# DLRM tower with compressed interaction layers: the first period in two halves of its samples

## The reference

```python
e = jnp.stack([tbl_f[ids[:, f]] for f in range(32)], axis=1)      # 1024 x 32 x 16
x0 = xk = e
for W in (W0, W1, W2):                                            # m x h x 64
    xk = jax.nn.relu(jnp.einsum('bmd,bhd,mhk->bkd', x0, xk, W))
    outs.append(jnp.sum(xk, axis=2))
h = jnp.concatenate([*outs, dense_ctx], axis=1)
h = relu(h @ W_top1 + b_top1); h = relu(h @ W_top2 + b_top2); y = h @ W_top3
```

## Time and profile before

| | |
|---|---|
| median of 3 runs | 638.52 us |
| the profiled execution | 638.18 us |
| its span, first to last instruction | 636.4 us |
| VectorE busy | 579.8 us, 309 instructions |
| TensorE busy | 584.7 us |
| GpSimd busy | 444.7 us, without the gaps between its gathers |
| ScalarE busy | 366.3 us |
| mean DMA rate | 166 GB/s |

### The profile page before, as it was taken

The page is one execution under the profiler, slowest core; times in us unless marked ns, Lnnn a source line. Parts: engine busy times, 40 slices in busy tenths (PEclk is TensorE's granted clock), DMA queues, the critical chain, the costliest instruction groups (busy, mean ns, idle before and its releaser), DMA issues.

```text
span 636.4 us, 7868 instructions
## 1 busy us (share of the span) xinstructions
PE 584.7 (92%) x2896; PEld 209.6 (33%) x2896; DVE 579.8 (91%) x309; ACT 366.3 (58%) x607; POOL 444.7 (70%) x416
## 2 busy tenths in 40 slices
PE   0078899999898989999999999999999999999998
PEld 0023233333232323333334323333334323334355
DVE  1039899999999999999999999999999999999995
ACT  0006474767656565747676575747676575737551
POOL 6677787698888878886979688886989582703012
PEclk9999999999999999999999999999999999999999
DMA  6296598938293845749291846648391946600000
GB/s 172 46 323 143 231 231 257 326 64 295 73 262 129 220 188 123 286 75 334 49 302 62 222 185 147 263 95 314 59 320 38 238 166 150 257 4 1 1 2 1
DMA packets 31315, 105.83 MB, mean 166 GB/s; under 512 B 8774, under 2 KB 14028, under 8 KB 27052
## 3 DMA queue, kind: packets, MB, share of 16 engines
q1 hardware_dynamic: 23084, 103.21, 51.6%
q0 software_dynamic: 8192, 2.11, 2.5%
HBM read 89.56 MB, written 15.73 MB: 165 GB/s over the span
## 4 chain that ended last, share of the span: by engine, by line
DVE 52%; PE 26%; issue 12%; DMA 5%; POOL 2%; SPq 1%; ACT 1%; DVEq 0%; ACTq 0%
DVE prod L555 51%; PE accb L648 9%; PE acca L648 8%; DMA rows<-field_dram 3%; POOL emb L417 2%; PE spread L691 2%; PE acc L605 2%; DMA field_dram<-zb_field 1%; PE accb L669 1%; PE acc L669 1%; SPq L318 1%; DVE prod L536 1%; PE spread L686 1%; ACT zb_field L778 0%; PE spread L612 0%
## 5 line engine op out<-in xcount | busy, mean ns | idle before, releaser
L417 POOL DMA_INDIRECT emb<-in_table,idx x256 | 246.4, 963 | 79.8 <-issue 67.8
L648 PE MATMUL acca<-prod,w 128*64 128x512 f32 x1024 | 229.1, 594 | 2.5 <-DVE prod L555 1.7
L648 PE MATMUL accb<-prod,w 128*64 128x512 f32 x960 | 216.1, 596 | 10.6 <-DVE prod L555 10.6
L555 DVE TENSOR_TENSOR prod<-rows,x1a 128x2048 f32<-128x2048 f32 x64 | 145.7, 2278 | 4.9 <-ACT x1a L783 2.5
L555 DVE TENSOR_TENSOR prod<-rows,x1b 128x2048 f32<-128x2048 f32 (+1 forms) x65 | 145.7, 2245 | 2.0 <-PE accb L648 1.4
L555 DVE TENSOR_TENSOR prod<-rows,x2a 128x2048 f32<-128x2048 f32 x64 | 145.6, 2278 | 0.8 <-PE accb L648 0.8
L555 DVE TENSOR_TENSOR prod<-rows,x2b 128x2048 f32<-128x2048 f32 x64 | 145.6, 2277 | 0.0
L648 PEld LDWEIGHTS acca<-prod,w 128*64 128x64 f32 x1024 | 71.7, 137 | 144.6 <-issue 134.3
L648 PEld LDWEIGHTS accb<-prod,w 128*64 128x64 f32 x960 | 65.8, 137 | 153.0 <-issue 113.7
L435 POOL TENSOR_TENSOR prod<-rows,mates 128x1024 f32<-128x1024 f32 x42 | 99.3, 2382 | 6.8 <-DMA rows<-field_dram 6.6
L783 ACT ACTIVATE x1a<-acc 64x512 f32<-64x512 f32 x62 | 35.3, 570 | 114.6 <-PE acc L605 113.9
(11 more groups left out here) (84 smaller groups left out, 309.3 us busy)
## 6 DMA issues: line engine op xcount, KB each, us to landing
rows<-field_dram SPq DMA_DIRECT2D x30, 2048.0 KB, 11.9
field_dram<-zb_field SPq DMA_DIRECT2D x32, 256.0 KB
mates<-field_dram SPq DMA_DIRECT2D x16, 512.0 KB, 4.4
across<-field_dram SPq DMA_DIRECT2D x56, 128.0 KB, 4.5
emb<-in_table,idx POOLq DMA_INDIRECT x256
field_dram<-zb_field SPq DMA_DIRECT2D x32, 128.0 KB
field_dram<-zb_field SPq DMA_DIRECT2D x16, 192.0 KB
rows<-field_dram SPq DMA_DIRECT2D x2, 1024.0 KB, 7.1
```

What stands on the lines that cost most here:

```text
L417: pool.indirect_dma_start(out=emb[q % EMBS][:, j * EMB:(j + 1) * EMB], out_offset=None, in_=table, in_offset=bass.IndirectOffsetOnAxis(ap= ...
L555: nc.vector.tensor_tensor(prod[:, n % RING, t:t + count, :], rows[:, at + t:at + t + count, c * HALF:(c + 1) * HALF], xs, ALU.mult).then_i ...
L648: mm = nc.tensor.matmul(acc[j % 2][side * HID:(side + 1) * HID, :], (w1 if layer == 1 else w2)[:, step, :], prod[:, (made(layer, s, half, ...
```

## The change

Period 0 is cut into two halves of 32 samples (`SPLITS`), each with all 16 `d`, in 512 columns. *Stream 0* and *stream 1* are now these halves. The ids and first rows of period 0 are laid out so that gathers 1 to 8 bring half 0 and 9 to 16 half 1. Each half has its own turning (`turn_first`, four products), copies out (`fields_first`), list (`list_eights`: eight DMAs of pieces of 512 B, four from SP and four from ScalarE's own queue), mates, rows (three DMAs) and five products of layer 0 (128 x 512). The index addition is split, period 0's first.

Slots 0 and 1 are gone: in their place stand 16 units (`FIRST_UNITS`) of one stream each, on TensorE as `outer_alone` in products of 256 columns. Slot 2 now holds (1, 2) and (1, 3); slots 3 to 31 hold what they held. The five products of period 1's layer 0 stand ahead of slot 2, and the turnings of periods 1 and 2 behind the 6th and the 16th unit. The layer 0 of period 2 is summed behind slot 2's last pair instead of in slot 2, that of period 3 one pair later than before; later ones are where they were. Idle products: six behind the first turning, two behind the second, five before slot 2. The host code lays out the ids; the arithmetic is the same. The diff, cut to its core (ScalarE's `split_twice`, `split_changed_over` and `split_by_d` do for a half of period 0 what the `relu_` functions do, in twice as many operations of 256 columns):

```diff
--- before.py
+++ after.py
...
+    SPLITS = 2
+    SPLIT = BT // SPLITS
+    FIRST_GATHERS = GATHERS // SPLITS
+    PIECE = QUAD * SPLIT
+    EIGHTS = [(first + e, 2 * half + j // 8 + e, step, times) for j, count, half, first, step, times in LIST_PARTS
+              for e in range(count // 8)]
...
-    FIRST = [(0, 2), (2, 2), (4, 1), (5, 3)]
+    FIRST = [(0, 2), (2, 3), (5, 3)]
...
+    FIRST_SLOT = 2
+    FIRST_UNITS = ([(1, 0, half, u) for half in range(2) for u in range(UNITS)] +
+                   [(2, 0, 0, u) for u in range(UNITS)] +
+                   [(1, 1, half, u) for half in range(2) for u in range(UNITS)] +
+                   [(2, 0, 1, u) for u in range(UNITS)] +
+                   [(2, 1, half, u) for half in range(2) for u in range(UNITS)])
     def streams(j):
-        if j == 0:
-            return [(1, 0), (1, 1)]
+        if j == FIRST_SLOT:
+            return [(1, j), (1, j + 1)]
         if j == SUBS - 1:
             return [(2, j - 1), (2, j)]
         return [(1, j + 1), (2, j - 1)]
...
-    MADE = [unit for j in range(SUBS) for unit in vector_units(j)]
+    MADE = FIRST_UNITS + [unit for j in range(FIRST_SLOT, SUBS) for unit in vector_units(j)]
...
-    FIELDS_AT = {(0, 3): 2}
-    SUM0 = {}
+    FIELDS_AT = {(FIRST_SLOT, 2): 3}
+    SUM0 = {(FIRST_SLOT, 3): [(k, 2) for k in (*range(L0 - 1), SQUARES, L0 - 1)]}
+    for q in range(4, PERIODS):
+        FIELDS_AT[2 * q - 5, 3] = q
     for q in range(3, PERIODS):
-        FIELDS_AT[2 * q - 5, 3] = q
-    for q in range(2, PERIODS):
-        SUM0[2 * q - 2, 0] = [(k, q) for k in range(3)]
-        SUM0[2 * q - 2, 1] = [(SQUARES, q), (L0 - 1, q)]
+        late = q == 3
+        SUM0[2 * q - 2, late] = [(k, q) for k in range(3)]
+        SUM0[2 * q - 2, 1 + late] = [(SQUARES, q), (L0 - 1, q)]
...
+        def list_eights(queue, h, odd):
+            for first, of, step, times in EIGHTS[odd::2]:
+                to = bass.AP(field_dram.tensor, (h * LENGTH + first * 8) * HALF,
+                             [[PIECE, FIELDS], [step * 8 * HALF, times], [1, PIECE]])
+                part = bass.AP(zb_field[:, :].tensor, FIELD * N + h * HALF + of * PIECE,
+                               [[N, FIELDS], [0, times], [1, PIECE]])
+                queue.dma_start(to, part).then_inc(s_listed_first[h], 16)
...
+            def list_first(h):
+                sp.wait_ge(s_field, h + 1)
+                list_eights(sp, h, 0)
+                sp.wait_ge(s_listed_first[h], len(EIGHTS) * 16)
+            def mates_first(h):
+                part = bass.AP(field_dram.tensor, (h * LENGTH + MATES) * HALF, [[HALF, P], [1, HALF]])
+                sp.dma_start(mates[:, h * HALF:(h + 1) * HALF], part).then_inc(s_mates, 16)
+            def rows_of_half(h, g):
+                t, count = FIRST[g]
+                part = bass.AP(field_dram.tensor, (h * LENGTH + t) * HALF, [[HALF, P], [1, count * HALF]])
+                sp.dma_start(rows_first[:, h, t:t + count, :], part).then_inc(s_first[h][g], 16)
...
-            list_fields(0)
-            mates_in(0)
-            for g, (t, count) in enumerate(FIRST):
-                spread_rows(0, t, count, s_first[g])
+            for h in range(SPLITS):
+                list_first(h)
+                mates_first(h)
+                for g in range(len(FIRST)):
+                    rows_of_half(h, g)
...
-            gather_early(0)
+            gather(0, 0, FIRST_GATHERS)
             pool.wait_ge(s_turned, 1)
+            gather(0, FIRST_GATHERS, FIRST_GATHERS)
+            pool.wait_ge(s_turned, SPLITS)
+            pool.wait_ge(s_at, 2)
             gather_early(1)
-            pool.wait_ge(s_l0, STEPS0)
+            pool.wait_ge(s_l0, steps_before(1))
...
+            def product_first(h, k):
+                t = EARLY_TILES[k]
+                if (h, k) == (0, 0):
+                    dve.wait_ge(s_at, 2)
+                if k == 0:
+                    dve.wait_ge(s_mates, (h + 1) * 16)
+                first_wait(h, t)
+                if k >= RING0:
+                    dve.wait_ge(s_l0, h * STEPS0 + k - RING0 + 1)
+                cols = slice(h * HALF, (h + 1) * HALF)
+                nc.vector.tensor_tensor(prod0[:, k % RING0, cols], rows_first[:, h, t, :], mates[:, cols],
+                                        ALU.mult).then_inc(s_prod0v, 1)
...
-                product0(0, k)
-            for j in range(SUBS):
+                product_first(0, k)
+            for i, unit in enumerate(FIRST_UNITS):
+                outer(*unit)
+                if i == 2 * UNITS - 1:
+                    for k in range(EARLY):
+                        product_first(1, k)
+            for k in range(EARLY):
+                product0(1, k)
+            for j in range(FIRST_SLOT, SUBS):
                 for unit in vector_units(j):
                     outer(*unit)
-                if j == 0:
-                    for k in range(EARLY):
-                        product0(1, k)
...
+            def turn_first(h):
+                wait_for(pe, s_field, h)
+                pe.wait_ge(s_gather[0], (h + 1) * FIRST_GATHERS * 16)
+                half = emb[0][:, h * FIRST_GATHERS * EMB:(h + 1) * FIRST_GATHERS * EMB]
+                by_d = half.rearrange("b (n d) -> b d n", d=QUAD)
+                for d in range(QUAD):
+                    mm = nc.tensor.matmul(spread[d * FIELDS:(d + 1) * FIELDS, h * P:(h + 1) * P], by_d[:, d, :], ident[:, :],
+                                          start=True, stop=True)
+                mm.then_inc(s_turned, 1)
...
+            def layer0_first(k, h):
+                pe.wait_ge(s_prod0v, h * EARLY + k + 1)
+                if (h, k) == (1, 0):
+                    pe.wait_ge(s_x1[1], 1)
+                    pe.wait_ge(s_z1a, 1)
+                for c in range(2):
+                    mm = nc.tensor.matmul(acc0[c * HID:(c + 1) * HID, h * PART:(h + 1) * PART], early_weights(k),
+                                          prod0[:, k % RING0, h * HALF + c * PART:h * HALF + (c + 1) * PART],
+                                          start=(k == 0), stop=(k == EARLY - 1))
+                mm.then_inc(s_l0, 1)
...
-            turn_fields(0, 0)
+            turn_first(0)
             pe.wait_ge(s_w12, 32)
-            pe.wait_ge(s_listed, len(LIST_PARTS) * 16)
-            keep_busy(acc[1][:, :], 5)
+            keep_busy(acc[1][:, :], 6)
+            turn_first(1)
+            keep_busy(acc[1][:, :], 2)
             pe.wait_ge(s_w0sum, 3)
-            for k in order0(0):
-                layer0(k, 0)
-            turn_fields(1, 0)
+            for k in range(EARLY):
+                layer0_first(k, 0)
+            for i, unit in enumerate(FIRST_UNITS):
+                outer_alone(*unit)
+                if i == 2 * UNITS - 1:
+                    for k in range(EARLY):
+                        layer0_first(k, 1)
+                if i == 3 * UNITS - 1:
+                    turn_fields(1, 0)
+            turn_fields(2, 0)
+            for k in order0(1):
+                layer0(k, 1)
+            pe.wait_ge(s_z3, 1)
             keep_busy(acc[1][:, :], 5)
             pe.wait_ge(s_top, 6 * 16)
             pe.wait_ge(s_ctx, 16)
-            towers, turned = 0, 2
-            for j in range(SUBS):
+            towers, turned = 0, turned_by(2)
+            for j in range(FIRST_SLOT, SUBS):
                 for i in range(2 * UNITS if j < SUBS - 1 else 4 * UNITS):
                     if j < SUBS - 1:
                         outer(j, i // UNITS, i % UNITS)
                     else:
-                        outer_alone(*vector_units(j)[i][1:])
-                    if (j, i) == (0, 2 * UNITS - 1):
-                        for k in order0(1):
-                            layer0(k, 1)
+                        outer_alone(*vector_units(j)[i])
                     if (j, i) in TOWER_AT:
                         g, stage = TOWER_AT[j, i]
                         tower_step(g, stage, turned)
...
                     if (j, i) in FIELDS_AT:
                         turn_fields(FIELDS_AT[j, i], towers)
                         turned += 1
-                    if (j, i) == (0, 2 * UNITS - 1):
-                        keep_busy(acc[1][:, :], 5)
-                    if (j, i) == (1, UNITS - 1):
-                        pe.wait_ge(s_field, turned)
-                        keep_busy(spread[:, :], 3)
                     for k, q in SUM0.get((j, i), []):
...
+            def fields_first(h):
+                act.wait_ge(s_turned, h + 1)
+                by_d = field[:, h * HALF:(h + 1) * HALF].rearrange("n (f d b) -> n d f b", f=BLOCKS, b=SPLIT)
+                turned = spread[:, h * P:(h + 1) * P].rearrange("q (f b) -> q f b", b=SPLIT)
+                for d in range(QUAD):
+                    last = nc.scalar.activation(by_d[:, d, :, :], turned[d * FIELDS:(d + 1) * FIELDS, :, :], ACT.Copy)
+                last.then_inc(s_field, 1)
+                act.wait_ge(s_field, h + 1)
+                list_eights(act, h, 1)
...
```

(46 more changed lines are left out.)

206 lines of the change are left out of this document (141 added, 65 removed).

## The result

The change takes **641.20 us**, the median of 5 runs (639.03 to 642.42); the kernel before, run beside it, takes 638.57 (638.24 to 638.60). The ratio is 1.0038 [1.0021, 1.0054]: 2.6 us slower. The forecast was 633.8, its range 630.5 to 638.0. The profiled execution is the fastest of the five, 639.03 us with a span of 637.2. It is 5.5 us above the 633.5 that the forecast's sum gives for a profiled execution, and all of this is lost before slot 2. The 2.2 us between it and the median have two sources, as far as the experiments show: the clock in slot 3, and the rows of period 1 (experiments 5 to 7).

What follows compares the result with a forecast made beforehand. VectorE, busy 91%, bounds the kernel, after waiting 33.95 us for its first rows. 16.3 won in front less 4.0, 4.85, 0.35, 0.67 and 1.7 makes 4.7: 633.5, by the median 633.8; range 630.5 to 638.0.

Steps and rivals of the forecast that it cites:

- Turning starts 2.35 later: Front: TensorE's turning starts 2.35 us after a half's last gather is issued; the second turning at 26.55.
- The clock rival: TensorE falls to its slow clock in a 3.4 us gap before the second turning; some 2.5 us, 636.3; chance 0.18.
- the bubble of 4.85 us: Where slots 2 and 3 meet: VectorE idles 4.85 us while TensorE's last pair and ScalarE's input finish.
- From here the slots are as before: After period 3's layer 0 in slot 5: nothing more is won or lost.
- the terms behind the first unit: Given back after the front: first period 4.0, slots 2 and 3 meeting 5.9, period 3's layer 0 1.7 us.
- the ring waits: VectorE's waits for the ring: 0.67 us comes again in slot 3; that of 0.84 is in both kernels.
- the wait for `x1a`: Slot 5: VectorE waits 1 to 2 us for this input, after period 3's later layer 0; 1.7 given back.
- The 0.35 for stream (1, 4): Slot 3: this stream's layer 0 stands behind the last pair, so its input comes at 108.4 against 108.05.
- the rival that made the change slower by slow pieces: At 167 ns a piece the first list lands at 28, first unit about 43, total 643 us; chance 0.13.
- layer 0 ends the wait before the first unit: Front: TensorE's layer 0, behind the idle products, ends the wait before the first unit, forecast at 33.0.
- My own bound: Forecast wrong if first unit is later than 36, the bubble is missing, or VectorE pauses again behind 150.
- the 1.7 given back for period 3: Slot 5: layer 0 one pair later on TensorE gives input at 144.5, while VectorE wants it at 142.9.

Runs made afterwards that it cites:

- experiments 5 to 7: The runs warm3, front_warm, warm_all and early1, which put idle products on TensorE in the change's gaps: 638.90, 639.66, 637.47 and 637.53 us.
- late_rows: The change with SP holding the second and third group of half 0's rows back until the second turning: 639.57 us, ratio 1.0010.
- free: The change with all 32 gathers in one run, two row groups held until half 1's gathers land, and idle products in front and slot 3: 634.93 us.
- no_pause: The change with GpSimd issuing both halves' 16 gathers without waiting for the first turning: 640.41 us, ratio 1.0017.
- no_pause_busy: no_pause with nine idle products instead of six behind the first turning: 640.82 us, ratio 1.0034.
- busy14: The change with fourteen idle products instead of six behind the first turning: 640.13 us, ratio 1.0027.
- warm3: The change with idle products in TensorE's two gaps of slot 3, four and two, front left alone: 638.90 us, ratio 1.0001.
- warm_all: warm3 with fourteen idle products instead of six behind the first turning and four more before the first unit: 637.47 us, ratio 0.9980.
- front_warm: warm_all without the idle products in slots 2 and 3: 639.66 us, ratio 1.0013.
- early1: warm_all with GpSimd gathering period 1 without waiting for the second turning: 637.53 us, ratio 0.9975.
- free_slot4: free with period 3's layer 0 summed one pair earlier, as for later periods: 633.33 us, ratio 0.9911.

## Why the prediction was wrong

- **The step that failed: "Turning starts 2.35 later" for the second half.** That figure is from a start in which nothing else ran on the DMA engines. In the change the first half's `mates` and `rows`, some 2.4 MB (512 KB and twice 768 KB of rows, 256 KB of mates), go out from 20.87 on, just where gathers 13 to 16 are issued. Landing took 5.71 us: 3.4 of the 3.7 us by which the turning was late; the last gather, 0.37 later than forecast, is the rest. I had priced these rows for VectorE, but not asked what they do to the gathers beside them. late_rows (2.52 with two groups of the rows held back) and free (3.29) show it; no_pause and no_pause_busy (6.8 and 6.7) show that an earlier issue alone hardly helps.
- **The clock rival's mechanism came true, at a gap of 7.8 us that I had not forecast.** I gave it 0.18 and 2.5 us of price, for a gap of 3.4. The two idle products cost 1.8 more (3.78 for 1.98) and layer 0 0.8 (34.59 to 37.55 is 2.96, for 2.15): 2.6, so the price was right; busy14, whose first unit comes 2.6 us sooner behind its turning than the change's, says the same. The Trainium skill ("TensorE: Matmul & The Clock Gate", Why this matters for your kernels) warns of idle gaps between bursts of matmuls; the granted clock of 0.50 bears it out. With both, the first unit is 6.2 late, and slot 2 5.7.
- **The step left out: what TensorE does in slot 3.** I took the bubble of 4.85 us as VectorE's alone. It is also a gap on TensorE (3.69, then 2.46), and the change removed the idle products of slots 0 and 1 without putting any there. The sentence "From here the slots are as before" holds, but the pairs in slot 3 are slower in some executions, which costs 1.3 us for one fall and 3.1 for both. The change's profiled run has no fall there, and a mean granted clock of 0.989; its four others, from 640.83 to 642.42, have 0.987, one step lower. That this step is a fall in slot 3 is inferred, since none of the four has a trace; warm3 against the change and warm_all against front_warm, 2.3 and 2.2 us lower by the medians, support it. One fall gives 1.3 of the 1.8 to 3.4 us by which they are longer. The pause for period 1's rows, absent from the one profile, can give the rest; no trace shows how it is shared.
- **Right:** the terms behind the first unit. Slot 2 comes 47.7 us after it (forecast 48.2, with period 1's rows binding; in this one profile they did not bind, in those of late_rows to early1 they did, and it is 48.6 to 50.3); the bubble is 4.94 (4.85), the ring waits 0.67 and 0.60 (0.67 and 0.84), the wait for `x1a` 1.79 (1.7). The 0.35 for stream (1, 4) did not show.
- **Right:** small pieces are not slow. The list, from its issue to that of `mates`, took 20.87 - 16.72 = 4.15 us, 4.7 forecast, with 179 and 188 GB/s in the two microseconds from 18; the rival that made the change slower by slow pieces (from 110 ns each) was wrong, and that the change came out slower, as it said, has another cause. (Its own sum is off as well: 49.32 - 43 is 6.3 won, which with 11.6 given back makes 643.8 and not 643.) The first products started at 25.19 (25.6).
- **Half right:** layer 0 ends the wait before the first unit, as forecast, but behind a late turning, not behind idle products on time.
- My own bound had said it: wrong if the first unit is later than 36. Put right, the terms nearly work: with the gathers landed first and no gap, free has the first unit at 34.56 and takes 634.9, 1.1 above the forecast of 633.8. Without the 1.7 given back for period 3 the forecast would have been 632.1, and free_slot4, which undoes that, is at 633.3, again 1.2 above. So the forecast was about the time of a kernel in which the first half's rows and the second half's gathers do not meet and TensorE has no gaps.

## What to carry to other kernels

When a stage is cut in two so that the halves overlap, list what runs on the DMA engines while the second half's small transfers are in flight: the first half's bulk loads now go out exactly then, and a latency read from the quiet start no longer holds. Hold the bulk back until the small transfers that others wait for have landed. And wherever a change moves a wait, look for the gap it opens on TensorE, and check whether the idle products that covered the old place have gone. One profile can be a lucky execution: compare its time and its granted clock with those of the other runs before reading what each wait costs.
